# Attention masks in a Trainium2 block: all mask tiles on GpSimd, the four tiles of a step in one instruction

## The reference, cut to what matters

```
q, k, v = heads(LN(x) @ Wq.T + bq), heads(ctx @ Wk.T + bk), heads(ctx @ Wv.T + bv)
scores  = q @ k.T / sqrt(32)
scores  = where(mask == 0, -1e9, scores) + attn_bias      # mask: per batch; bias: per head
x       = x + (softmax(scores) @ v) @ Wo.T + bo
```

## Time and profile before

| | |
|---|---|
| median of 3 runs | 1891.92 us (1888.12 to 1892.15) |
| profiled execution, its own time | 1890.4 us |
| its span | 1888.5 us |
| PE busy | 1818.5 us, 96% |
| DVE busy | 1037.1 us, 55% |
| ACT busy | 793.8 us, 42% |
| POOL busy | 888.1 us, 47% |

### The profile page before, as it was taken

How to read it: one execution, slowest core, us unless ns; L and a number is a source line. 1 busy time by engine, 2 the same in 40 slices (tenths; PEclk the granted TensorE clock), 3 DMA queues, 4 the chain that set the end, 5 groups by cost and what they waited for, 6 DMA issues and landing times.

```text
span 1888.5 us, 31571 instructions
## 1 busy us (share of the span) xinstructions
PE 1818.5 (96%) x11736; PEld 1358.6 (72%) x11736; DVE 1037.1 (55%) x2401; ACT 793.8 (42%) x1720; POOL 888.1 (47%) x702
## 2 busy tenths in 40 slices
PE   6999998999999999999699999999999999999998
PEld 5888886555555555555477888888888888888886
DVE  5555555998998999899654422433233342332411
ACT  3222223888888888888331211312112131221310
POOL 1211214999999999999213232232322413223211
PEclk9999998999999999999889999999999999999999
DMA  8888888626245335431433463554535555355453
GB/s 298 286 302 313 311 314 310 244 96 224 91 135 178 137 115 174 147 115 36 143 116 101 150 213 123 179 189 163 195 122 189 188 170 190 121 198 177 150 188 114
DMA packets 198007, 340.11 MB, mean 180 GB/s; under 512 B 10464, under 2 KB 52064, under 8 KB 197344
## 3 DMA queue, kind: packets, MB, share of 16 engines
q1 hardware_dynamic: 194592, 325.50, 50.7%
q0 software_dynamic: 3264, 12.58, 1.9%
HBM read 268.84 MB, written 69.21 MB: 179 GB/s over the span
## 4 chain that ended last, share of the span: by engine, by line
PE 49%; DVE 2%; ACT 1%; issue 0%; POOL 0%; DVEq 0%; ACTq 0%
PE n_ps_y L1459 18%; PE n_ps_h L1440 18%; PE n_ps_m L1376 9%; PE n_ps_y L1376 2%; PE n_ps_m L1370 1%; DVE n_aT_l L1080 0%; DVE h_bias L1180 0%; DVE n_stats L1093 0%; DVE h_k L1180 0%; DVE h_bias L1152 0%; DVE n_g_h L1234 0%; DVE k_az L1105 0%; DVE k_x L1226 0%; DVE h_k L1161 0%; POOL n_rstd L1043 0%
## 5 line engine op out<-in xcount | busy, mean ns | idle before, releaser
L1062 POOL TENSOR_TENSOR n_g_l<-h_pos,n_g_h 128x512 fp32r<-128x512 f32 x128 | 186.4, 1456 | 581.3 <-DVE n_g_h L1234 581.3
L863 ACT ACTIVATE a_t_s<-a_t_s,a_nmax 128x512 f32<-128x512 f32 x512 | 364.4, 715 | 15.8 <-DVE a_nmax L812 15.8
L1440 PE MATMUL n_ps_h<-n_zT_h,n_w 128*128 128x512 f32 x1024 | 338.5, 392 | 2.1 <-DVE n_r_row L1210 2.1
L812 DVE CUSTOM_DVE_ANT_0 a_t_s<-a_ps_s,a_t_s 128x512 f32<-128x512 f32 x464 | 295.2, 687 | 44.8 <-PE a_ps_s L722 27.9
L733 PEld LDWEIGHTS a_ps_t<-ident,a_t_s 128*128 128x128 f32 x2048 | 221.3, 142 | 136.7 <-issue 108.8
L694 POOL TENSOR_TENSOR a_t_s<-a_pos,a_bias_t 128x512 f32<-128x512 f32 x256 | 317.8, 1271 | 0.2
L1459 PE MATMUL n_ps_y<-n_w,n_g_h 128*128 128x512 f32 x1024 | 316.6, 390 | 0.0
L1332 ACT ACTIVATE h_pos<-n_ps_h 128x512 f32<-128x512 f32 x128 | 75.5, 596 | 535.4 <-PE n_ps_h L1440 535.4
L733 PE MATMUL a_ps_t<-ident,a_t_s 128*128 128x128 f32 x2048 | 281.6, 281 | 0.3 <-ACT a_pT L850 0.3
L1234 DVE CAST n_g_h<-h_pos 128x512 fp32r<-128x512 f32 x128 | 55.8, 436 | 374.2 <-ACT h_pos L1332 374.2
L1440 PEld LDWEIGHTS n_ps_h<-n_zT_h,n_w 128*128 128x128 f32 x1024 | 193.3, 189 | 42.5 <-DVE n_r_row L1210 2.5
(11 more groups left out here) (165 smaller groups left out, 2652.1 us busy)
## 6 DMA issues: line engine op xcount, KB each, us to landing
n_w<-wf_d SPq DMA_DIRECT2D x256, 512.0 KB, 4.2
a_pos<-pos_d SPq DMA_DIRECT2D x24, 1024.0 KB, 6.3
a_bias_t<-in_bias POOLq DMA_DIRECT2D x9, 1024.0 KB, 7.2
p_c_raw<-in_ctxT SPq DMA_DIRECT2D x8, 1024.0 KB, 8.0
p_x_raw<-in_x SPq DMA_DIRECT2D x8, 1024.0 KB, 10.3
p_m_raw<-in_mask SPq DMA_DIRECT2D x8, 1024.0 KB, 12.7
k_d<-p_k_s SPq DMA_DIRECT2D x8, 1024.0 KB, 12.1
pos_d<-p_pos SPq DMA_DIRECT2D x8, 1024.0 KB, 10.5
```

The lines of the kernel that those rows point to most:

```text
L812: dve.tensor_tensor_reduce(t_s[:, j % NN, i:i + 1, :], ps_s[:, i:i + 1, :], added, 1.0, 3.0e38, ALU.add, ALU.min, nmax[:, j % NN, i:i + 1] ...
L863: act.activation(t_s[:, j % NN, i, :], t_s[:, j % NN, i, :], ACT.Exp, scale=-1.0, bias=nmax[:, j % NN, i:i + 1], accum_out=total[:, j // 2 ...
L1062: pool.tensor_tensor(out=g_l[:, f % NG, :], in0=g_f[:, f % NG, :], in1=g_h[:, f % NG, :].bitcast(F32), op=ALU.subtract).then_inc(g_low, 1)
L1440: last = pe.matmul(ps_h[:, f % 2, :], stationary, moving, start=i == 0, stop=i == len(passes) - 1)
```

## The change

VectorE makes no mask tile any more. GpSimd makes all four of a step, and from the second step of the stage on it makes them in one instruction over 128x2048 elements: pos is read four times by a stride of zero, and the wait and the count are those of all four tiles. The first step keeps four instructions of one tile.

```
-    DVE_NBM = (1, 3, 5, 7, 9, 11)
+    DVE_NBM = ()
...
-                for i in range(HG):
-                    if nbm_by_dve(j, i):
-                        continue
-                    pool.wait_ge(turned, tiles((g, j)) + i + 1)
-                    pool.tensor_tensor(out=t_s[:, j % NN, i:i + 1, :], in0=pos_rows(b, qt, qt + 1), in1=bias_rows(i, i + 1, qt),
-                                       op=ALU.subtract).then_inc(nbm_pool, 1)
+                n = HG - nbm_by_dve(j, HG - 1)
+                for first, end in ((0, n),) if g + j else ((i, i + 1) for i in range(n)):
+                    pool.wait_ge(turned, tiles((g, j)) + end)
+                    pool.tensor_tensor(out=t_s[:, j % NN, first:end, :],
+                                       in0=pos_rows(b, qt, qt + 1).broadcast_to([P, end - first, S]),
+                                       in1=bias_rows(first, end, qt), op=ALU.subtract) \
+                        .then_inc(nbm_pool, end - first)
```

## The result

The changed kernel takes 1894.21 us (median of 17 runs, 1891.76 to 1897.92), the kernel before in the same comparison 1890.83 (17 runs). The ratio is 1.0020, with a 95% interval of 1.0012 to 1.0027: slower by 0.2%, 3.4 us by the medians. The profiled execution took 1895.94 us, its span is 1894.1.

The account below looks back on a forecast made before the run. GpSimd was taken to bind the attention: +9.1 us on its own time and -1.7 us at the stage's end give +7.4 on the profiled 1890.4 us, with the median 1.5 higher; forecast 1898 us, range 1886 to 1908.

Parts of the forecast that it names:

- What bounds: Attention: GpSimd, never waiting for a ring slot, sets the pace; a head group's 148.0 us is its time.
- The case that I forecast: Attention: GpSimd's fused instructions at a pitch of 4.52 to 4.60 us make the kernel slower, 1894 to 1904 us; chance 0.58.
- T: Attention: pitch of GpSimd's fused 128x2048 mask instruction, put at 4.55 us, from readings of 4.52 to 4.57.
- no difference: Rival: pitch between 4.46 and 4.52 us, dropped overhead just pays for the tiles taken over, about 1892 us; chance 0.25.
- The eightfold row: Trace rows of a 128x2048 subtraction into fp32r, 4624 ns eight times, used as a reading of the fused instruction's duration.
- GpSimd's sum: Attention: GpSimd's time from first mask start to last mask end, 588.25 us before and 597.3 after, +9.1 us.
- 14.5 us of stops: GpSimd's bias loads, 13.9 us, and first bias wait, 0.55 us, taken to remain unchanged.
- lag: Stage end: last step's reductions start 0.2 us after GpSimd's end where it was 1.88, so -1.7 us.
- The ring: GpSimd's added wait for all four tiles of a slot to be transposed: 6.5 us of lead left, cost zero.
- VectorE's relief: The 48 subtractions leaving VectorE save its chain 1.7 us a head group, worth nothing while GpSimd alone binds.
- Cheap fusion: Rival: fused instruction's pitch is 4.41 us, the attention gets 6.6 us faster, 1884 us; chance 0.12.
- the split by the zero stride: Rival: hardware does the fused instruction as four full-cost pieces, 4.95 us, +58 us, 1948 us; chance 0.05.

Follow-up runs that it names:

- eight: The kernel before, with only its bias loads moved from GpSimd to SyncE: 1884.80 us against 1890.92.
- two: The changed kernel, but GpSimd makes all four mask tiles in an instruction each, VectorE none: 1943.76 us, ratio to before 1.0282.
- six: The changed kernel, but the fused instruction writes fp32r, so mask tiles are rounded: 1894.12 us in one run.
- one: The changed kernel with fused GpSimd instructions, but VectorE keeps its 6 mask tiles a round: 1887.47 us against 1890.24 before.
- nine: Probe: the changed kernel, GpSimd making only three of four mask tiles a step from the second round, the fourth left out: 1880.84 us against 1892.19 before.
- five: The changed kernel, but the fused instruction reads four different rows of pos in place of one by zero stride: 1895.58 us in one run.
- three: The changed kernel, with the next head group's bias loads issued by SyncE and none by GpSimd: 1879.35 us against 1890.24 before.
- seven: The changed kernel with two GpSimd instructions of two tiles a step in place of one of four: 1910.58 us against 1890.92 before.

## Why the prediction was right, and where its size was off

**What bounds.** GpSimd binds the stage before: shown from both sides, since eight takes 4.6 us off the stage by freeing GpSimd of DMA issues alone, and two adds GpSimd's 58.9 us almost whole.

**Direction.** Of the two parts, the takeover costs +54.5 us of stage by itself and fusion gives -2.1 by itself (then the other lane binds), but together they leave +4.2. The forecast was +7.4, 1898 us, against 1894.21 measured, +3.4 by the medians. The case that I forecast came, by its sign and its mechanism. By T it came at its very edge, since the case began at 4.52 and the rival "no difference" ended there. The difference is also below the 0.2%, 3.8 us, that I had called indistinguishable from none. That it fell on the forecast's side is in part luck; the interval and the stage's own +4.2 decide it.

**The term that was mis-sized** is T, the pitch of the fused instruction. I took 4.55 between two readings, 4.52 from the single 4572 ns row and 4.57 from the eightfold 4624 ns row, and it is 4.52. That is 127 x 0.029 = 3.7 us too much. The single row alone would have given the right value. The step from duration to pitch was right: I took off 0.052 us, and 4.567 - 4.521 = 0.046 was measured. The eightfold row came from another stage, where the same size takes longer; six shows that its output type was not the reason. The first bias wait gave 0.7 of this back. So GpSimd's sum was 597.3, and 594.15 was measured; the next terms held: 14.5 us of stops, lag 0.17 for 0.2. The head group that starts at 462.84 takes 149.2 us for the 150.2 that I gave.

**The ring.** I worked out 6.5 us as the lead that GpSimd may have. In one, where it stands at the ring's end, the lag of the last step is 6.2. With three tiles, in nine, 13.6 - 2.5 - 3.5 = 7.6 is due and 7.7 was measured.

**VectorE's relief** was put at no value under a binding GpSimd. The changed kernel bears this out: VectorE is idle 98.0 us ahead of its 512 reductions where it had 59.0: 44.8 ahead of the 464 that read GpSimd's tile and 14.2, nearly all of it waiting for its own subtraction, ahead of the 48 others. I had expected the waits to stand under GpSimd's name, but most stand under the scores':

```profile
DVE a_t_s L813 <- PE a_ps_s L723: 62.3, 58, 3.4
DVE a_t_s L813 <- POOL a_t_s L693: 21.9, 12, 5.0
```

The 12 waits for GpSimd, 21.9 us, are at the stage's start (3) and around the bias stops (9). In between the chain needs 4.52 itself, so it really waits for scores in every second step, and only 0.17 us for masks in the other. My T of 4.55 made GpSimd bind throughout; with 4.52 both lanes are even between the bias stops.

**The rivals.** Cheap fusion (T = 4.41) and the split by the zero stride (4.95) didn't come; five leaves no effect of the stride above 7 ns. The bound given with the first of them, that even a free GpSimd brings no more than about 10 us, held: nine takes 9.5 us off the stage. "No difference" (T up to 4.52) is closest: the measured ratio lies at the line of 0.2% that I had drawn, and its interval excludes 1. The Trainium skill ("GPSIMD Engine Reference", section 3.1) has 4497 ns for the add of 2048 elements; the duration of the subtraction here is 4560 to 4572, so the measurement stands. The same section measures about 2.6 cycles an element for GpSimd, and section 1 gives it a clock of 1.2 GHz. From these I estimate 2.17 ns an element, and the slope of 2.14 ns here agrees.

**What I left out** is the point of the case: the stops at the bias loads were in my sum as a constant, 14.5 us "as does their cause". They are the reason why GpSimd, level with the chain at 4.52 a step, still binds. In the changed kernel they are worth 13 us (three), three times what the change itself moves, and they set its sign: with the stops in neither kernel the change gains 4.3 us.

## What to carry to other kernels

When two engines run at nearly the same pace, count each over a whole period, with the stops that come once in it. Here the stops decided who binds, and the cheapest gain was to move the DMA issues off the binding engine's queue. Fusing GpSimd's instructions was worth here their number times a fixed cost; measure that cost by a line through two sizes, and weigh it against the work that is moved along with it. A fused producer also hands over later. Here this cost something only at the two ends of the stage: 2.8 us at its end where the producer binds (two), and about 1.8 us at its start where the reader binds (one against eight).

## What the runs showed of the hardware that I had not expected

GpSimd's two-input subtraction keeps to a line of 0.14 us and 2.14 ns an element from 512 to 2048, within 7 ns whatever the stride of the operand and the output type at 2048 (two, seven, after, five and six).

The changed kernel's 17 runs spread over 6 us, and their mean granted TensorE clock goes with it: 1891.76 us at 0.992, 1897.92 at 0.985. In the profiled run after, the 2.5 us behind the attention go with a stretch in the third stage at the lower of the two clocks (1.2 and not 2.4 GHz). From 998.20 to 1005.00 the granted clock is 0.50, half of full speed:

```profile
989.02:999.02 10.00, 7.08 (x33) 5.53 (x31) 8.63 (x19) 3.19 (x5) 2.20 (x1) 0.96 0.59 200
999.02:1009.02 10.00, 10.00 (x36) 8.35 (x37) 6.78 (x7) 2.42 (x5) 8.95 (x6) 0.70 0.18 63
```

In the kernel before, the same work (4.1 us earlier) ran at a granted clock of 1.00:

```profile
984.91:994.91 10.00, 7.08 (x32) 5.53 (x31) 8.64 (x19) 3.19 (x5) 2.20 (x1) 1.00 0.60 195
994.91:1004.91 10.00, 8.87 (x42) 7.19 (x43) 6.39 (x7) 2.32 (x5) 8.95 (x6) 1.00 0.20 69
```

The first row of each pair ends at the same eight transposes, and what TensorE had done before them is the same: 7.08 us of matmuls, then 2.92 us of idle time. The clock fell in the one and not in the other, and the eight transposes took 1.97 us in place of 1.10. The profiled runs of the other kernels have such a stretch or not, and their time behind the stage is 984.7 to 988.2 us. So a difference of 2 us between two single profiles says nothing of the change; the medians and the stage's own time do.
